# An attention and mixture-of-experts kernel: a tile's weights travel in its gathered rows instead of by a gather of their own, and the adding scatter drops one of its waits

## The reference

```python
x = x + layernorm(attention(layernorm(x), ...))     # 16 heads of 16, 4 batches of 1024 tokens, rotary positions
xs = layernorm(x)                                    # (4096, 256)
dist = sqrt(max(|xs|^2 + |centroid|^2 - 2 xs @ centroid.T, 1e-12))   # 8 experts
w, sel = top_k(dist, 2);  w = softmax(w)             # two experts a token, two weights
for e in range(8):
    h = silu(xs @ Wg[e] + bg[e]) * (xs @ W1[e] + b1[e])     # 256 -> 684
    out = out + we[:, e:e+1] * (h @ W2[e] + b2[e])          # 684 -> 256
x = x + layernorm(out)
```

## Time and profile before

| | |
|---|---|
| median of three runs | 1604.24 us (1593.34 to 1605.25) |
| profiled execution, its own time | 1608.56 us |
| its span, first to last instruction | 1605.8 us |
| mean granted clock of TensorE | 0.943 |
| busy: TensorE, VectorE, ScalarE, GpSimd | 86%, 70%, 60%, 39% of the span |

### The profile page before, as it was taken

How to read it: one execution, slowest core, us unless ns; L and a number is a source line. 1 busy time by engine, 2 the same in 40 slices (tenths; PEclk the granted TensorE clock), 3 DMA queues, 4 the chain that set the end, 5 groups by cost and what they waited for, 6 DMA issues and landing times.

```text
span 1605.8 us, 31875 instructions
## 1 busy us (share of the span) xinstructions
PE 1377.3 (86%) x10413; PEld 876.6 (55%) x10414; DVE 1116.9 (70%) x1890; ACT 958.9 (60%) x1755; POOL 629.6 (39%) x464
## 2 busy tenths in 40 slices
PE   7899999999999999999998439888888888888860
PEld 5454433343333334343454228878878888778860
DVE  6998999999999999995045675455445544554444
ACT  4523888888888878888734324444444444444435
POOL 4750033121313222224123044555555555555545
PEclk9998999999999999999968759999999999999995
DMA  6985357566565646650467714444444444444556
GB/s 210 268 217 101 89 116 184 167 175 187 88 185 92 152 66 155 97 117 12 126 116 198 283 69 140 120 106 111 119 120 110 107 120 120 110 109 118 161 143 209
DMA packets 181488, 220.39 MB, mean 137 GB/s; under 512 B 57583, under 2 KB 152748, under 8 KB 178837
## 3 DMA queue, kind: packets, MB, share of 16 engines
q1 hardware_dynamic: 165493, 200.52, 47.0%
q0 software_dynamic: 15904, 18.66, 6.6%
HBM read 146.64 MB, written 72.48 MB: 136 GB/s over the span
## 4 chain that ended last, share of the span: by engine, by line
DVE 38%; PE 28%; DMA 16%; issue 13%; POOL 2%; ACT 1%; DVEq 1%; SPq 0%; POOLq 0%; ACTq 0%
DVE mx L1094 25%; DMA w_slot<-w_d,at_w 13%; PE psum L1707 4%; PE psum L1680 4%; DVE psum L1087 3%; PE psum L1871 3%; PE psum L1694 2%; DVE h_lo L1327 2%; PE psum L1781 2%; PE psum L1852 2%; PE psum L1854 2%; PE psum L1853 2%; PE psum L1640 2%; DMA y_d<-values,at_y 2%; PE psum L1654 2%
## 5 line engine op out<-in xcount | busy, mean ns | idle before, releaser
L1478 ACT ACTIVATE work<-psum 128x512 f32<-128x512 f32 x1024 | 543.7, 600 | 93.7 <-PE psum L1694 69.0
L1094 DVE TENSOR_REDUCE mx<-psum 128x1 f32<-128x1024 f32 (+1 forms) x512 | 546.8, 1097 | 24.4 <-PE psum L1680 11.1
L1680 PE MATMUL psum<-stack 48*128 48x512 f32 x1024 | 377.4, 450 | 21.3 <-DVE mx L1094 10.9
L1694 PE MATMUL psum<-stack 50*128 50x512 f32 x1024 | 375.8, 451 | 0.0
L1680 PEld LDWEIGHTS psum<-stack 48*128 48x128 f32 x1024 | 162.1, 187 | 262.2 <-DVE mx L1094 169.0
L1707 PE MATMUL psum<-work,values 128*32 128x384 f32 x4080 | 304.4, 394 | 0.2
L955 POOL DMA_INDIRECT values<-xn_d,at_x x71 | 149.1, 2100 | 221.6 <-DVE at_w L1344 208.1
L1317 DVE COPY small<-w_slot 128x1 f32 (+1 forms) x71 | 10.9, 154 | 266.9 <-DMA w_slot<-w_d,at_w 266.9
L1852 PE MATMUL psum<-w_hi,x_hi 128*128 x568 | 188.7, 332 | 1.8 <-DVE x_lo L1312 1.0
L1853 PE MATMUL psum<-w_lo,x_hi 128*128 x568 | 182.3, 321 | 0.0
L1854 PE MATMUL psum<-w_hi,x_lo 128*128 x568 | 182.2, 321 | 0.0
(11 more groups left out here) (201 smaller groups left out, 2059.4 us busy)
## 6 DMA issues: line engine op xcount, KB each, us to landing
stack<-qk_scr SPq DMA_DIRECT2D x192, 128.0 KB, 6.1
work<-in_w SPq DMA_DIRECT2D x36, 640.0 KB
small<-in_w SPq DMA_DIRECT2D x35, 640.0 KB
qk_scr<-weights SPq DMA_DIRECT2D x16, 1024.0 KB, 4.7
split_raw<-in_w SPq DMA_DIRECT2D x8, 1368.0 KB
wh_d<-w_hi SPq DMA_DIRECT2D x6, 1368.0 KB, 5.8
w_hi<-wh_d SPq DMA_DIRECT2D x6, 1368.0 KB, 13.0
ot_scr<-weights SPq DMA_DIRECT2D x16, 512.0 KB, 3.2
```

The source lines that it names most:

```text
L1094: dve.tensor_reduce(mx[:, r, a, t:t + 1], scored, AX, ALU.max, negate=True).then_inc(s_max, 1)
L1478: act.activation(pt[u % 4][:, j, :], bank((c + HG * u + n) % 3), ACT.Exp, scale=SC).then_inc(s_exp, 1)
L1680: ins = pe.matmul(bank(4 + 2 * a + half), qs[t3][at:at + QROWS, r, P * t:P * (t + 1)], ks[t3][at:at + QROWS, r, 512 * half:512 * (half + 1 ...
L1694: pe.matmul(bank((t3 + HG * u + n) % 3), ks[t3][at:at + MROWS, r, P * st:P * (st + 1)], qs[t3][at:at + MROWS, r, 512 * half:512 * (half + ...
```

## The change

The two weights of a token are written into two more columns of its row of `xn2_d` (now 258 wide), so that the row gather brings them; VectorE multiplies them by a pair of zeros and ones by slot (`choice`, made in the routing by two more steps) and adds the two. `w_d`, its stores, TensorE's and ScalarE's turn of the weights, the weight gather and its index go. SP stores the pairs (4096 pieces of 8 bytes) once they are ready, ahead of the high weights of experts 4 to 6. In SP's list of the projection stage the stores of `x2` and the high weights of experts 0 and 1 stand later. GpSimd's scatter no longer waits for the transposes of the rows of a later tile. With a tile's weights in the row, `keep_weight` is behind `pick_weight` and `aim_gather`.

```diff
-        w_both = sb("w_both", [P, 2, NT])
-        w_1, w_2 = w_both[:, 0, :], w_both[:, 1, :]
-        w_slot = sb("w_slot", [P, 1])
+        choice = dots_sb[:, 27:, :].rearrange("p n c -> p (n c)")[:, 0:2 * NS].rearrange("p (s a) -> p s a", a=2)
+        w_pair = sb("w_pair", [P, NT, 2])
+        w_1, w_2 = w_pair[:, :, 0], w_pair[:, :, 1]
+        w_slot = sb("w_slot", [P, 2])
-        x_row = [c.take([C]) for _ in range(2)]
+        x_row = [c.take([C + 2]) for _ in range(2)]
-        xn2_d = nc.dram_tensor("xn2_d", (NTOK, C), F32, kind="Internal").ap()
+        xn2_d = nc.dram_tensor("xn2_d", (NTOK, C + 2), F32, kind="Internal").ap()
-        w_d = nc.dram_tensor("w_d", (2 * NTOK + P, 1), F32, kind="Internal").ap()
@@ SP, projection stage
-                if u % 2 == 1:
-                    store_x2(u // 2)
-                if u in (2, 3):
-                    load_high(sp, u - 2)
+                for m in {8: (0, 1), 9: (2, 3), 10: (4,), 11: (5,), 13: (6,), 15: (7,)}.get(u, ()):
+                    store_x2(m)
+                if u in (12, 14):
+                    load_high(sp, u // 2 - 6)
...
             sp.wait_ge(s_x2s, 16 * (NT // 4))
+            sp.wait_ge(s_w12, 1)
+            sp.dma_start(xn2_d.rearrange("(n p) c -> p n c", p=P)[:, :, C:], w_pair[:, :, :]).then_inc(s_wd, 16)
             for e in range(4, E - 1):
                 load_high(sp, e)
-            sp.wait_ge(s_wc, 1)
-            sp.dma_start(w_d[0:2 * NTOK, :].rearrange("(a p) o -> a (p o)", p=P), w_turned).then_inc(s_wd, 16)
-            sp.wait_ge(s_wd, 32)
@@ GpSimd
             def scatter(t, p):
-                if not isinstance(t, int) or t + 4 <= NS:
-                    pool.wait_ge(s_mt, t + 4)
...
                     gather(t + 3, 1 - p)
-                if not isinstance(t, int) or t + 2 < NS:
-                    gather_weight(t + 2)
@@ VectorE
+            step(dve.tensor_scalar(choice[:, :, 0], place_of[:, :], float(NTOK), None, ALU.is_lt))
+            step(dve.tensor_scalar(choice[:, :, 1], place_of[:, :], float(NTOK), None, ALU.is_ge))
...
+            def pick_weight(t, p):
+                after(dve, s_wk, 2 * t)
+                dve.tensor_tensor(w_slot[:, :], x_row[p][:, C:C + 2], choice[:, bass.ds(t, 1), :].rearrange("p s a -> p (s a)"),
+                                  ALU.mult).then_inc(s_wk, 1)
+
             def keep_weight(t):
-                dve.wait_ge(s_wg, 16 * (t + 1))
-                dve.tensor_copy(w_all[:, bass.ds(t, 1)], w_slot[:, :]).then_inc(s_wk, 1)
+                dve.wait_ge(s_wk, 2 * t + 1)
+                dve.tensor_tensor(w_all[:, bass.ds(t, 1)], w_slot[:, 0:1], w_slot[:, 1:2], ALU.add).then_inc(s_wk, 1)
...
                     low_x(t + 1)
-                    keep_weight(t + 1)
+                    pick_weight(t + 1, 1 - p)
                 if not isinstance(t, int) or t + 3 < NS:
                     aim_gather(t + 3, 1 - p)
-                if not isinstance(t, int) or t + 2 < NS:
-                    aim_weight(t + 2)
+                if not isinstance(t, int) or t + 1 < NS:
+                    keep_weight(t + 1)
@@ ScalarE, TensorE
-            act.wait_ge(s_wt, 1)
-            act.activation(w_turned, bank(6)[0:2 * NT, 0:P], ACT.Copy).then_inc(s_wc, 1)
-            pe.wait_ge(s_w12, 1)
-            pe.transpose(bank(6)[0:2 * NT, 0:P], w_both[:, :, :].rearrange("p a n -> p (a n)"), ident[:, :]).then_inc(s_wt, 1)
```

More of the change, by code:

```diff
@@ L267, in build @@
         dots_sb = small[:, C + B * P:].rearrange("p (n c) -> p n c", c=32)
-        w_turned = dots_sb[0:2 * NT, 0:P // 32, :].rearrange("a n c -> a (n c)")
         w_all = dots_sb[:, 24:24 + -(-NS // 32), :].rearrange("p n c -> p (n c)")
@@ L271, in build @@
         cent_t = sb("cent_t", [P, KC, 32])
-        w_both = sb("w_both", [P, 2, NT])
-        w_1, w_2 = w_both[:, 0, :], w_both[:, 1, :]
-        w_slot = sb("w_slot", [P, 1])
+        choice = dots_sb[:, 27:, :].rearrange("p n c -> p (n c)")[:, 0:2 * NS].rearrange("p (s a) -> p s a", a=2)
+        w_pair = sb("w_pair", [P, NT, 2])
+        w_1, w_2 = w_pair[:, :, 0], w_pair[:, :, 1]
+        w_slot = sb("w_slot", [P, 2])
         row_of = sb("row_of", [P, NS])
-        at_w = sb("at_w", [P, 1], I32)
         token_of = sb("token_of", [P, NS])
@@ L397, in build @@
         s_w12 = sem("weights_of_choices_ready")
-        s_wt = sem("weights_of_choices_turned")
-        s_wc = sem("weights_of_choices_copied")
         s_wd = sem("weights_of_choices_stored")
-        s_iw = sem("weight_gather_aimed")
-        s_wg = sem("slot_weights_gathered")
-        s_wk = sem("slot_weights_kept")
+        s_wk = sem("slot_weight_step")
         s_bh = sem("slot_tiles_compared")
@@ L636, in _ @@
                 sp.dma_start(x_all[:, 8 * m:8 * m + 8, :], x_v[:, 8 * m:8 * m + 8, :]).then_inc(s_x[m + 1], 16)
-            sp.wait_ge(s_zero, 1)
-            sp.dma_start(w_d[2 * NTOK:, :].rearrange("(a n) o -> a (n o)", a=1), zeros[0:1, 0:P]).then_inc(s_wd, 16)
             for w in range(4):
@@ L965, in scatter @@
                                         in_=y_row[p], in_offset=None, compute_op=ALU.add).then_inc(s_ys, 16)
[L967 to L972, removed]
             for b in range(2 * NT // 4):
@@ L982, in _ @@
                 pool.wait_ge(kept_of, 16 * NT // 8)
-            pool.wait_ge(s_wd, 32)
+            pool.wait_ge(s_wd, 16)
             def tile(t, p):
@@ L989, in tile @@
                     gather(t + 3, 1 - p)
-                if not isinstance(t, int) or t + 2 < NS:
-                    gather_weight(t + 2)
             gather(0, 0)
             gather(1, 1)
-            gather_weight(0)
             gather(2, 0)
-            gather_weight(1)
             for t in range(2):
@@ L1340, in aim_scatter @@
                 dve.tensor_copy(at_y[:, :], row_of[:, bass.ds(t, 1)]).then_inc(s_is, 1)
-            def aim_weight(t):
-                after(dve, s_wg, 16 * t)
-                dve.tensor_copy(at_w[:, :], place_of[:, bass.ds(t, 1)]).then_inc(s_iw, 1)
             def tile(t, p):
@@ L1369, in _ @@
             aim_gather(1, 1)
-            aim_weight(0)
             low_x(0)
+            pick_weight(0, 0)
+            aim_gather(2, 0)
             keep_weight(0)
-            aim_gather(2, 0)
-            aim_weight(1)
             for t in range(4):
@@ L1573, in save_y @@
                 after(act, s_ys, 16 * (t - 1))
-                act.wait_ge(s_wk, t + 1)
+                act.wait_ge(s_wk, 2 * t + 2)
                 act.activation(y_row[p], bank(7)[:, 0:C], ACT.Copy, scale=w_all[:, bass.ds(t, 1)]).then_inc(s_yr, 1)
```

## The result

The changed kernel ran at 1477.97 us, the median of four runs (1476.41 to 1481.67); the kernel before, four runs on the same chip, at 1603.12. The ratio is 0.923, interval 0.918 to 0.928. The forecast was 1512, the range 1496 to 1548: the direction was right, the gain came out larger than the range allowed. The profiled execution took 1476.41 us, its span is 1474.5, against 1605.8 before; these 131.3 us are accounted for here.

What follows compares the result with a forecast made beforehand. The prediction took the weight-gather ring, 8.41 us a tile, as the bound; -83.3 (TensorE idle), -9.9 (projection) and +0.5 (routing) sum to -92.7, so 1608.56 becomes 1515.9, or 1512 against the median; range 1496 to 1548.

Steps and rivals of the forecast that it cites:

- the projection stage: SP's later x2 stores and high weights remove norm_o's wait near 860 and the slow clock behind it: -9.9 us, bounds -4 and -9.9.
- The ring: Per tile: VectorE's weight copy, GpSimd's row gather, weight gather and its landing, 8.26 us; the change breaks it, TensorE then bounds.
- Rivals 1 and 4: First: new TensorE gap, 0.3 to 0.7 us a tile, 1540, chance 0.20; second: VectorE still waits for row gather, 1600, 0.03.
- rival 3: Expert tiles: each scatter's index waits for the previous scatter to land, 9.04 us a tile, 1634 in all; chance 0.04.
- The pace of TensorE: Tiles 2 to 64: TensorE needs 7.07 to 7.09 us a tile, so only its idle time goes, -83.3 us.
- the "gapless" tile: Tile from 968.30 to 975.37 in the old profile, read as 7.07 us of TensorE without a wait.
- Tiles 65 to 68: Last expert tiles, beside the reads of x2: no gain taken, bounds 0 and -5.3 us.
- the two steps of `choice`: Routing: two more VectorE steps on the path before the gathers, +0.5 us.
- Rival 2: Projection stage gains nothing because the loads themselves fill the queues until 860 or later: 1522, chance 0.10.
- The pair store: Before the experts: store of 4096 8-byte pieces lands in 7.4 us, high loads behind it arrive in time, cost 0.
- Rival 5: The store of weight pairs holds the first expert tile up by 10 us: 1522, chance 0.03.
- The scatter's wait: GpSimd's scatter in the expert tiles: dropping its wait for the row transposes was said to cost and gain 0.

## Why the prediction was wrong, by its steps

Two terms were too small: the idle time taken off for tiles 2 to 64, -83.3 where -102.2 was measured, and the projection stage, -9.9 where the first gather came 24.5 us earlier, 12.4 of them by a chance state of the clock and not by the change. The first alone, put right, would have made the forecast 1493, already below the range.

**The ring goes, TensorE becomes the bound: right.** After the change VectorE waits for no DMA, TensorE is busy for all of tiles 2 to 64, the slack of `h_lo` is 1.22 us for the 1.3 laid out, and doubling `low_w2` overdraws it by about the difference. Rivals 1 and 4 are out; so is rival 3, since neither the index nor anything else waits for `y_d` there, though the DMA share is 0.53. The gather became shorter, as was said, 0.99 us.

**The pace of TensorE, 7.07 to 7.09 us a tile: wrong, and the larger error (18.9 us).** The prediction took as gain only TensorE's idle time, 83.3 us, so it took the busy time of a tile with a stall for the time of a tile without one. The 18.9 us come apart like this: 61 stalls at 0.26 us are 15.9, worked out from the groups above. The remaining 3 us are two short pieces at half clock around 1150 and 1269 in the kernel before (granted clock 0.77 and 0.83 in windows of 5 us), which the prediction kept; after has 1.00 throughout. The page TensorE: Matmul & The Clock Gate of the Trainium skill, section Single matmul latency, gives a single bf16 product at full clock a constant of about 166 ns on top of the time of its columns. The 0.16 us by which the first group runs longer is of that size, but these products are fp32r and their ends are modelled, so it proves nothing.

The prediction's second reading of the pace, the "gapless" tile, could have shown this. It confirmed the 7.07 instead, by a slip: it ends one product too late. In the kernel before

```profile
968.31 0.42 PE L1852 MATMUL psum<-w_hi,x_hi 128*128 x1
...
975.12 0.40 PE L1852 MATMUL psum<-w_hi,x_hi 128*128 x1
975.36 0.32 PE L1853 MATMUL psum<-w_lo,x_hi 128*128 x1
```

the tile runs from first product to first product, 968.31 to 975.12, 6.81 us; the window of the earlier trace rows ended at 975.36, the second product. The tile at 1539.61 likewise ends at 1546.44, 6.83 us. With 6.81 the same sum would have given 530.07 less 429.0, or -101.

**Tiles 65 to 68: taken as 0, they brought 4.6 of the bound of 5.3.** TensorE's idle time there fell from 5.3 to 1.8 us under the same reads, and the busy time by 1.1. Of the 5.3 us, 3.8 were waits for `h_lo`, so most of those stalls were the same ring.

**The projection stage: the mechanism right, the size off (15.1 us with what follows).** The first gather moved by 24.5 us, which three comparisons of the same instant take apart: 954.04 to 941.63 with no edit, 12.4, the slow stretch that the first profile happened to have; 941.63 to 928.80 with SP's order, 12.8; 928.80 to 929.50 for the two steps of `choice` with the rest of the change, +0.7 (0.5 was said). The term was -9.9 because the wait in that profile was 5.86 us. At full clock GpSimd comes to the same loads 15.4 us sooner (843.77 against 859.19), and they land only 10.6 us sooner (854.46 against 865.05), so it waits 10.69. The forecast read the wait's length as a property of the kernel, when a chance state of the clock had shortened it. Rival 2 is out: the wait went whole.

**The pair store: right.** It was issued at 890.32 and landed after 7.8 us (7.4 was estimated; the high loads behind it were early enough, and the first tile didn't wait for them). The Trainium skill, DMA: Bandwidth & Descriptors, section Specifications, says that below 512 bytes the DMA engine reads, modifies and writes, but gives no price; the doubling to 14.8 us was the prediction's own guess, and it is not in that 7.8. The row that the 7.4 came from had pieces of 32 bytes, so it had any such cost in it already. Rival 5 is out. The wider rows cost GpSimd nothing: a row gather holds it 0.99 us, where it was 2.16 before.

**The scatter's wait: right**, 0 both ways. What went on TensorE and ScalarE in the routing can't be told from nothing in these runs, as was said.

## What to carry to other kernels

Before moving data to save a tiny transfer, look at what stands ahead of it in its queue: here an exchange of two neighbouring DMAs broke the ring for the same gain as carrying the weights in the rows. When a stall goes, take off more than its idle time, since the busy time around it shrinks too; read the pace of a bound engine from an unstalled tile, from the first instruction to the same instruction of the next. And before a wait for a load is priced from one profile, look at the granted clock ahead of it: here a slow stretch delayed the engine that waits by 15.4 us and the load by 10.6, and so hid part of the wait.

## What was not expected of the hardware

- With a stall of 0.49 us in each tile the tiles grew by 0.75 us; in the other 0.26 TensorE counts as busy.
- The granted clock fell to 0.50, 1.2 GHz, for 30.7 us at about 797 with TensorE busy for all of it, in some executions and not in others of the same code, and in one for 78.5 us from 96.2 on. Ahead of the first the two profiles of the same kernel show the same work. What decides it stays open; it goes with 12.4 us at the first gather, and with differences of 15 us between runs.
- An indirect gather held GpSimd 2.16 us on average in the kernel before and 0.99 in the changed one, for rows that are even 8 bytes wider. Groups of each kernel, tiles 2 to 64, before and then after:

```profile
L955 POOL DMA_INDIRECT values<-xn_d,at_x x63 | 135.8, 2155 | 195.2 <-DVE at_w L1344 187.1 <-issue 8.1
```

```profile
L946 POOL DMA_INDIRECT values<-xn_d,at_x x63 | 62.3, 988 | 20.1 <-issue 20.1
```

That it would be shorter was expected, that it would be less than half was not. What changed is what runs beside it, and two runs show it apart from the change. Doubling `low_w2` in the changed kernel, the only edit, took the mean from 0.99 to 2.39 us (first group below). There, as in the earlier trace rows, the gather is issued while `low_w2` (L1319 here) is at work. With the scatter's wait put back, `low_w2` (L1320) starts inside the gather, and the gather keeps its 0.99 us (63 such gathers, none over 1.00):

```profile
L947 POOL DMA_INDIRECT values<-xn_d,at_x x54 | 129.0, 2389 | 16.5 <-issue 16.5
```

```profile
1201.13 1.76 DVE L1319 TENSOR_TENSOR w_lo<-work,w_hi 128x1536 fp32r<-128x1536 f32 x1 [1.47 <-ACT w_hi L1549]
...
1201.28 2.47 POOL L947 DMA_INDIRECT values<-xn_d,at_x  x1 [0.30 <-issue]
```

```profile
1208.77 0.99 POOL L946 DMA_INDIRECT values<-xn_d,at_x  x1 [0.30 <-issue]
...
1209.18 1.76 DVE L1320 TENSOR_TENSOR w_lo<-small,w_hi 128x1536 fp32r<-128x1536 f32 x1 [1.89 <-ACT w_hi L1548]
```

In the earlier trace rows `low_w2` ends at 1308.26 and the gather at 1309.12; in the doubled kernel the first `low_w2` ends at 1202.89 and the gather at 1203.75, both 0.86 us later. So it is a gather issued while `low_w2` runs that is held, until 0.86 us behind its end. Why is not shown. The ring of the earlier trace rows contained this hold, about 1.0 us of its 8.26 (an estimate, 2.00 less 0.99).
